# A state-space block with a gated feed-forward on one core: one pair of input terms on GpSimd, ten decay tiles, a moved silu, a transposed residual

## The chip, the cores and the metric

The kernel runs on one core of a Trainium2 chip. The metric is the device time of one launch in microseconds (us); lower is better. Five engines work in parallel, each in its own program order and tied to the others by semaphores: TensorE (PE, matmuls), VectorE (DVE), ScalarE (ACT, activations), GpSimd (POOL), and SyncE (SP), which here only issues DMAs.

## The reference

Input x is 32 sequences of 256 steps with 128 channels, all in float32.

```python
xz = x @ W_in.T                      # 128 -> 512, halves x_ssm and z (256 channels each)
x_ssm = silu(conv4(x_ssm) + conv_b)  # causal, one 4-tap filter for each channel
proj = x_ssm @ W_x.T                 # 16 columns B, 16 columns C, 1 column dt
dt = softplus(proj[..., -1:] * W_dt[:, 0] + b_dt)
h_t = exp(dt_t * A) * h_{t-1} + (x_t * dt_t) * B_t      # 256 channels x 16 states
y_t = sum over states of h_t * C_t, plus x_t * D
attn = (y * silu(z)) @ W_out.T
x1 = layernorm(x + attn)
h = silu(lin(x1, w1)) * lin(x1, w2)  # 128 -> 512
h = gelu(lin(h, h1)); h = gelu(lin(h, h2))              # 512 -> 512, twice
out = layernorm(x1 + lin(h, w3))     # 512 -> 128
```

## The kernel before

**Blocks and rounds.** Two sequences make one block of 512 columns (TB), 16 blocks in all. The program is a software pipeline of 18 rounds j, written out by hand in `rounds` (L212). In round j the scan of block j runs (DVE, POOL, ACT), beside it the front of block j+1 (z, silu of the convolution, rows of B and C, dt), the intake of block j+2 (projection and convolution), the back of block j-1 (output projection, first norm, gate and up, first hidden layer) and the tail of block j-2 (second hidden layer, down projection, second norm). Each engine's `run` walks through 16 visits v and has its instructions hung on a visit; that list is the order of its queue. Rounds 2 to 14 hold every part; round 0 has no back, round 1 no tail, round 15 no front, round 16 no scan, and round 17 is tail alone.

**The scan.** 256 channels times 16 states are 32 tiles u of 128 partitions, two for each visit. A group k is four tiles and takes one load of dt (`dtr`) and one of x*dt (`xdr`), spread from DRAM over the partitions by SP; neighbouring groups share a load, so k=1 and k=3 use the same one, and only the first of them waits for it. B is spread into `brep`, and ACT copies it into the PSUM bank X (`fill_X`, L438), three times in a round. For tile u:
- ACT forms the decay `dA` = exp(dt*A) (`decay`, L425), into a ring of 8 tiles, six tiles ahead of the scan (DA_RING, AHEAD, L33 and L36).
- DVE forms the input term U = X * xdr (L723) in one of two PSUM banks and then scans, h = dA*h + U (L736), into `hb`, a ring of four pairs (the wait on s_p, L731).
- POOL multiplies the pair of `hb` by C into `pb`, also four pairs (`output_term`, L368).
- PE sums four tiles over the states into Y (`sum_group`, L801), once in two visits: group k after visit 2k+1 of POOL, in PE's visit 2k+3.

In round 0 the first three groups take their replicated dt and x*dt from PE (`replicate`, L870, matrix `rep_sb`) and not from DRAM.

**The rest of a round, where the change touches it.** POOL's visit 4 begins with the reciprocal root of the first norm (`rsqrt`, L379), visits 7 and 8 with the products silu(gate)*up (L408, two in each), visits 9, 11 and 12 with the terms of dt (`add_dt`, `times_dt`). DVE's visit 0 has the three taps of the convolution's first half, visit 1 the gate of the former block's second half (it needs PE's sum of group 7), visit 5 x1 (`scaled`, L683), visit 10 the gate of the first half. ACT's visit 1 has two gelus, the start of Y and then `silu_conv` (L456), which needs the silu table and after which the exp/log table is loaded again (L612); visit 3 has the variances of the first norm; visit 6 the silus of the four gates with the copies of the four ups (L633 to L639); visit 7 the copy of the rows and the softplus for dt. PE's visit 4 has `add_x1` (L837), which puts x1T times the centring matrix `cent` into the bank of the down projection, `turn_x1` (L864, transposes of x1) and `down`; visit 6 the first gate and up matmuls; visit 8 `rows_proj` and `dt_proj`, which need the silu of the convolution. `down_last` (L827) does for the last block what `add_x1` and `down` do for the others.

Of the kernel before, what the change touches and what calls it, by code (L numbers as in the profile page):

```python
# [24 lines left out]
GT = 4  # L25
# [4 lines left out]
PARITIES = 2  # L30
LOADS = NC * PARITIES
DT_SLOTS, XD_SLOTS = LOADS, 3
DA_RING = 8  # L33
H_PAIRS = 4
P_PAIRS = 4
AHEAD = 6  # L36
EPS = 1e-5

CW, CB, DP, WD, BD = 0, 4, 5, 6, 7
CHP = 8  # L40


def states_of(k):

    return (0, 0, 1, 1, 1, 1, 0, 0)[k]


def build(nc, xT, win, wx, chp, alog, cwrow, sel, rep, wout, w1, w2, h1, h2, w3, scales, cent_in, ident_in, out):
    with ExitStack() as ctx:
# [20 lines left out]
        sc_sb = sb("sc_sb", [P, 5, NH])  # L70
        negA = sb("negA", [P, TILES])
        sel_sb = sb("sel_sb", [P, PARITIES, 2 * SD])
        rep_sb = sb("rep_sb", [P, PARITIES, P])
        diagD = sb("diagD", [P, NC, P])
        ident, cent = sb("ident", [P, P]), sb("cent", [P, P])
        mhalf, eps = sb("mhalf", [P, NT]), sb("eps", [P, NT])

# [25 lines left out]
        hid = sb("hid", [P, NH, TB])  # L103
        g1 = sb("g1", [P, NH, TB])
        up = g1
        g2 = hid
        yo = sb("yo", [P, NT, DM])
        w3_raw = yo[:].rearrange("p a b -> p (a b)")
# [31 lines left out]
        s_rdt, s_rxd = sem("s_rdt"), sem("s_rxd")  # L140
        s_X, s_start = sem("s_X"), sem("s_start")
        s_dA, s_u, s_h, s_p, s_y = sem("s_dA"), sem("s_u"), sem("s_h"), sem("s_p"), sem("s_y")
        s_gate, s_op = sem("s_gate"), sem("s_op")
        s_var1, s_rs1, s_x1, s_x1t, s_x1c = sem("s_var1"), sem("s_rs1"), sem("s_x1"), sem("s_x1t"), sem("s_x1c")
        s_ga, s_sg, s_up, s_upc, s_hid = sem("s_ga"), sem("s_sg"), sem("s_up"), sem("s_upc"), sem("s_hid")
# [76 lines left out]
        def _(sp):  # L222
# [13 lines left out]
            def spread_B(b, g):  # L236
                if b > 0:
                    sp.wait_ge(s_X, 3 * b - g)
                piece = scr_rows[b % 2, g * SN:(g + 1) * SN, :]
                sp.dma_start(brep[:, g, :], piece.unsqueeze(0).to_broadcast([SD, SN, TB])).then_inc(s_b[g], 16)  # L240

# [8 lines left out]
                    sp.dma_start(o[:, slot, q, :], piece.unsqueeze(1).to_broadcast([SD, SN, TB])).then_inc(s_o[slot][q], 16)  # L250

            load_xT(0)
            sp.dma_start(rep_sb[:], rep).then_inc(s_rep, 16)
            sp.dma_start(wc1[:], cwrow.to_broadcast([P, TAPS * P])).then_inc(s_cw, 16)
            sp.dma_start(wx_sb[:], wx.rearrange("(c p) m -> p c m", p=P)).then_inc(s_wx, 16)
            sp.dma_start(ident[:], ident_in).then_inc(s_ident, 16)
# [36 lines left out]
            def run(j, scan, intake, front, back, tail):  # L293
                I, A, F, T = j + 2, j + 1, j - 1, j - 2
                if scan:
                    if j > 0:
                        sp.wait_ge(s_dA, TILES * j)
                        spread_steps(j, 1, 1, scr_dt, dtr, s_dtr)
                        sp.wait_ge(s_u, TILES * j)
                        spread_steps(j, 1, 0, scr_xd, xdr, s_xdr)  # L300
                    if back:
                        sp.wait_ge(s_op, F + 1)
                    sp.dma_start(xres[:], xT[:, bass.ts(j, TB)]).then_inc(s_xres, 16)
                if intake:
                    sp.wait_ge(s_c1, A + 1)
                    sp.wait_ge(s_z, 2 * A + 2)
                    load_xT(I)
                if scan and j > 0:
                    sp.wait_ge(s_u, TILES * j + 3 * GT)
                    spread_steps(j, 1, 1, scr_xd, xdr, s_xdr)  # L310
                if front:
                    sp.wait_ge(s_rows, A + 1)
                    store_rows(A, range(NT))
                    sp.wait_ge(s_dt, 2 * A + 1)
                    store_steps(A, 0, scr_dt, dts, s_dts)
                    sp.wait_ge(s_xd, 2 * A + 1)
                    store_steps(A, 0, scr_xd, xds, s_xds)
                    sp.wait_ge(s_dts[0], 16 * (A + 1))
                    sp.wait_ge(s_dA, TILES * j + 4 * GT)
                    spread_steps(A, 0, 0, scr_dt, dtr, s_dtr)  # L320
                    sp.wait_ge(s_store, 16 * NT * (A + 1))
                    spread_B(A, 0)
                    sp.wait_ge(s_xds[0], 16 * (A + 1))
                    sp.wait_ge(s_u, TILES * j + 4 * GT)
                    spread_steps(A, 0, 0, scr_xd, xdr, s_xdr)
                    spread_steps(A, 0, 1, scr_dt, dtr, s_dtr)
                    spread_C(A, (0,))
                    sp.wait_ge(s_dt, 2 * A + 2)
                    store_steps(A, 1, scr_dt, dts, s_dts)
                    sp.wait_ge(s_xd, 2 * A + 2)  # L330
                    store_steps(A, 1, scr_xd, xds, s_xds)
                    sp.wait_ge(s_u, TILES * j + 7 * GT)
                    spread_steps(A, 0, 1, scr_xd, xdr, s_xdr)
                    spread_B(A, 1)
                    spread_C(A, (1,))
                if tail:
                    rows_out = out[bass.ts(T, TB), :].rearrange("(t p) m -> p t m", p=P)
                    sp.wait_ge(s_yo, T + 1)
                    if j <= NB:
                        sp.dma_start(rows_out, yo[:]).then_inc(s_out, 16)  # L340
                    else:
                        sp.dma_start(rows_out[:, 0:2, :], yo[:, 0:2, :]).then_inc(s_out, 16)
                        sp.wait_ge(s_yo, T + 2)
                        sp.wait_ge(s_yoa, 1)
                        sp.dma_start(rows_out[:, 2:4, :], yo[:, 2:4, :]).then_inc(s_out, 16)
                if front:
                    sp.wait_ge(s_dts[1], 16 * (A + 1))
                    sp.wait_ge(s_dA, TILES * j + 7 * GT)
                    spread_steps(A, 1, 0, scr_dt, dtr, s_dtr)
                    sp.wait_ge(s_xds[1], 16 * (A + 1))  # L350
# [5 lines left out]
        def _(pool):  # L356
# [11 lines left out]
            def output_term(b, v):  # L368
# [3 lines left out]
                if v >= P_PAIRS or b > 0:  # L372
# [3 lines left out]
                nc.gpsimd.tensor_tensor(pb[:, qs:qs + 2, :], hb[:, hs:hs + 2, :],  # L376
                                        crep[:, b % 2, g:g + 1, :].to_broadcast([P, 2, TB]), ALU.mult).then_inc(s_p, 1)

            def rsqrt(var, ve, rs, s_var, n_var, s_rs, n_rs, ts=slice(0, NT)):  # L379
                pool.wait_ge(s_var, n_var)  # L380
                nc.gpsimd.tensor_tensor(ve[:, ts], var[:, ts], eps[:, ts], ALU.add).then_inc(s_rs, 1)
                pool.wait_ge(s_rs, n_rs - 1)
                nc.gpsimd.tensor_tensor(rs[:, ts], ve[:, ts], mhalf[:, ts], ALU.pow).then_inc(s_rs, 1)
# [12 lines left out]
            def run(j, scan, intake, front, back, tail):  # L396
                I, A, F, T = j + 2, j + 1, j - 1, j - 2
                for v in range(STEPS):
# [16 lines left out]
                        add_dt(A, 1)  # L415
                    if v == 12 and front:
                        times_dt(A, 1)
                    if scan:
                        output_term(j, v)

# [3 lines left out]
        def _(act):  # L424
            def decay(b, u):  # L425
# [6 lines left out]
                    act.wait_ge(s_dtr[slot][q], 16 * loads_up_to(b, k, DT_SLOTS))  # L432
                if u >= DA_RING or b > 0:
                    act.wait_ge(s_h, TILES * b + u - DA_RING + 1)
                nc.scalar.activation(halves(dA[:, u % DA_RING, :])[:, :, 1:SEQ], halves(BREP[q] if by_product(b, k) else dtr[:, slot, q, :])[:, :, 1:SEQ],  # L435
                                     ACT.Exp, scale=negA[:, u:u + 1]).then_inc(s_dA, 1)

            def fill_X(b, i):  # L438

                g = i % 2  # L440
                if i < 2:
                    act.wait_ge(s_b[g], 16 * (b + 1))
                if b > 0 or i > 0:
                    act.wait_ge(s_u, TILES * b + (0, 2 * GT, 6 * GT)[i])
                nc.scalar.activation(X[:], brep[:, g, :], ACT.Copy).then_inc(s_X, 1)  # L445

            def conv_first(b):
# [112 lines left out]
            def run(j, scan, intake, front, back, tail):  # L560
# [3 lines left out]
                for v in range(STEPS):  # L564
# [41 lines left out]
                        copy_z(A, 0)  # L606
                    if v == 4 and tail:
                        gelu(g2, 3, BH2, s_h2, s_g2, T, (2, 3))
                    if v == (1 if back else 5) and front:
                        silu_conv(A, 0)  # L610
                        silu_conv(A, 1)
                        act.preload_act_table_set("natural_log_exp_and_others")  # L612
# [5 lines left out]
                    if v == 6:  # L618
# [4 lines left out]
                        if j == NB + 1:  # L623
# [6 lines left out]
                                    last.then_inc(s_var2, 1)  # L630
                            act.wait_ge(s_rs2, 2 * T + 4)
                            nc.scalar.activation(yo[:, 3, :], BLAST[3][:, 0:P], ACT.Copy, scale=rs2[:, 3:4]).then_inc(s_yoa, 1)
                        for m in range(NH) if back else ():  # L633
                            act.wait_ge(s_ga, 4 * F + 1 + m)
                            nc.scalar.activation(hid[:, m, :], BGATE[m], ACT.Silu,  # L635
# [27 lines left out]
        def _(dve):  # L663
# [37 lines left out]
            def run(j, scan, intake, front, back, tail):  # L701
                I, A, F, T = j + 2, j + 1, j - 1, j - 2
                for v in range(STEPS):
                    if scan:
# [6 lines left out]
                            dve.wait_ge(s_X, 2)  # L711
                        elif v in (0, 4, 12):
                            dve.wait_ge(s_X, 3 * j + 1 + (0, 4, 12).index(v))
                        for i in range(2):
                            if v > 0 or j > 0:
                                dve.wait_ge(s_h, TILES * j + 2 * v + i - 1)
                            if by_product(j, k):
# [14 lines left out]
                        for i in range(2):  # L732
                            u = 2 * v + i
                            dve.wait_ge(s_dA, TILES * j + u + 1)
                            dve.wait_ge(s_u, TILES * j + u + 1)
                            nc.vector.tensor_tensor_scan(hb[:, 2 * (v % H_PAIRS) + i, :], dA[:, u % DA_RING, :], U[i][:],  # L736
                                                         0.0, ALU.mult, ALU.add).then_inc(s_h, 1)
                    if v == 4 and j == 0:
                        taps(1)
# [19 lines left out]
        def _(pe):  # L759
# [66 lines left out]

            def down_last(b):  # L827
                for t in range(NT):
                    nc.tensor.matmul(BLAST[t][:, 0:P], tile_of(x1T[:], t), cent[:], start=True, stop=False, skip_group_check=True)
                pe.wait_ge(s_g2, 4 * b + 4)  # L830
                for t in range(NT):
                    for k in range(NH):
# [4 lines left out]
            def add_x1(b):  # L837

                pe.wait_ge(s_g2, 4 * b + 3)
                for t in range(NT):  # L840
                    nc.tensor.matmul(tile_of(BW3, t), tile_of(x1T[:], t), cent[:], start=(t == 0), stop=False, skip_group_check=True)

            def down(b):
                pe.wait_ge(s_w3c, 1)
# [238 lines left out]
```

## Time and profile before

| | |
|---|---|
| runs shown | 1063.3, 1059.74, 1062.15 us (median 1062.15) |
| profiled execution, its own time | 1063.54 us |
| span in the profile | 1061.7 us, 13755 instructions, so 1.8 us lie around it |
| busy, share of the span | PE 95%, DVE 90%, ACT 86%, POOL 75% |
| mean granted TensorE clock | 0.969 of full speed |
| table loads on ACT | 1283 ns each |
| DMA | 184 MB, mean 173 GB/s |

A busy share is a mean over the launch. PE's times are modelled at their ends: two matmuls in a row overlap a little in the records, so a merged row of the timeline is a little longer than the distance to the next row's start. The work of a stretch is best read from start to start. A row `[1.33 <-POOL pb L376]` says how long the engine had stood idle before the row and who, by the profile, released it; where an instruction waits for several semaphores the named one is only the last by the profile.

### The profile page before, as it was taken

The numbers are of one execution on the slowest core, as the hardware profiler recorded it, in microseconds if no ns is written. First come the engines' busy times: TensorE is split into PE (matmuls) and PEld (weight loads), VectorE is DVE, ScalarE is ACT, GpSimd is POOL, SyncE is SP. The second block draws the span as 40 slices with busy tenths as digits, with TensorE's granted clock in tenths as the row PEclk, the third lists the DMA queues.
The fourth block names the chain that finished last, engine by engine and source line by source line (L and its number), as shares of the span: only waits on it lengthen the run. The fifth ranks groups of instructions, "written<-read, shape, count | busy, mean of one in ns | idle before, by whom it ended". The sixth has DMA issues, their size and how long they took to land.

```text
span 1061.7 us, 13755 instructions
## 1 busy us (share of the span) xinstructions
PE 1006.7 (95%) x4000; PEld 457.4 (43%) x4000; DVE 952.1 (90%) x1143; ACT 909.6 (86%) x1519; POOL 796.1 (75%) x455
## 2 busy tenths in 40 slices
PE   5947999999999999999999999999999999999998
PEld 2313335353444535353443535344453535335454
DVE  1899999999999999999999999999999999999500
ACT  5396798999999999999999999999999999996442
POOL 1476877969787896969788796978789696977520
PEclk8677899999999999999999999999999999998999
DMA  4959294764939286583929377482928658391000
GB/s 128 280 183 285 66 282 121 220 209 122 258 97 300 85 248 179 164 249 101 295 63 300 117 225 204 132 248 94 316 71 246 181 172 233 98 295 50 1 10 11
DMA packets 110428, 184.14 MB, mean 173 GB/s; under 512 B 12944, under 2 KB 23696, under 8 KB 110352
## 3 DMA queue, kind: packets, MB, share of 16 engines
q1 hardware_dynamic: 109824, 182.94, 59.2%
q8 instruction: 32, 0.52, 0.2%
q14 instruction: 44, 0.36, 0.1%
q10 hardware_dynamic: 528, 0.32, 0.1%
HBM read 161.19 MB, written 22.02 MB: 173 GB/s over the span
## 4 chain that ended last, share of the span: by engine, by line
PE 56%; POOL 14%; issue 13%; DVE 9%; ACT 7%; DMA 0%; POOLq 0%; ACTq 0%; SPq 0%; DVEq 0%
PE G L818 21%; PE Y L809 7%; POOL pb L376 6%; PE G L848 5%; PE G L769 5%; DVE hb L736 5%; PE Y L818 5%; POOL hid L408 3%; DVE U L723 3%; PE G L822 3%; PE Y L860 2%; ACT dA L435 2%; POOL dts L359 2%; POOL xds L366 2%; PE G L825 1%
## 5 line engine op out<-in xcount | busy, mean ns | idle before, releaser
L376 POOL TENSOR_TENSOR pb<-hb,crep 128x1024 f32<-128x1024 f32 x256 | 603.2, 2365 | 177.6 <-DVE hb L736 154.3
L736 DVE TENSOR_TENSOR_SCAN hb<-dA,U 128x512 f32<-128x512 f32 x512 | 594.5, 1203 | 21.1 <-POOL pb L376 18.5
L435 ACT ACTIVATE dA<-dtr,negA 128x510 f32<-128x510 f32 x500 | 320.8, 711 | 1.6 <-DVE hb L736 1.1
L723 DVE TENSOR_TENSOR U<-X,xdr 128x512 f32<-128x512 f32 x500 | 318.3, 683 | 0.7 <-ACT X L445 0.7
L818 PE MATMUL G<-g,h_sb 128*128 128x512 f32 x512 | 234.2, 601 | 0.0
L818 PE MATMUL G<-hid,h_sb 128*128 128x512 f32 x384 | 173.1, 601 | 0.8 <-ACT g L638 0.8
L809 PE MATMUL Y<-pb,sel_sb 128*32 128x512 f32 x1024 | 139.1, 615 | 17.6 <-POOL pb L376 17.6
L818 PEld LDWEIGHTS G<-g,h_sb 128*128 128x128 f32 x512 | 93.5, 190 | 138.2 <-issue 136.5
L818 PEld LDWEIGHTS G<-hid,h_sb 128*128 128x128 f32 x384 | 70.4, 190 | 103.8 <-issue 101.9
L408 POOL TENSOR_TENSOR hid<-hid,g 128x512 f32<-128x512 f32 x64 | 80.8, 1274 | 14.6 <-ACT g L638 14.6
L809 PEld LDWEIGHTS Y<-pb,sel_sb 128*32 128x32 f32 x1024 | 20.7, 109 | 96.8 <-issue 71.9
L769 PE MATMUL G<-xT_sb,wc 128*128 128x512 f32 (+3 forms) x120 | 58.6, 634 | 2.8 <-ACT w_sb L592 2.3
L517 ACT ACTIVATE hid<-G,sc_sb 128x512 f32<-128x512 f32 x64 | 42.4, 686 | 20.9 <-PE G L818 20.4
L517 ACT ACT_TABLE_LOAD x45 | 57.7, 1283 | 0.8
L848 PE MATMUL G<-w_sb,hid 128*128 128x128 f32 x480 | 58.2, 281 | 0.0
L818 PE MATMUL Y<-hid,h_sb 128*128 128x512 f32 x128 | 57.5, 592 | 0.0
L848 PEld LDWEIGHTS G<-w_sb,hid 128*128 128x128 f32 x480 | 57.1, 198 | 0.0
L635 ACT ACTIVATE hid<-G,sc_sb 128x512 f32<-128x512 f32 x48 | 32.9, 686 | 26.8 <-PE G L822 26.8
L822 PE MATMUL G<-x1T,w_sb 128*128 128x512 f32 x96 | 51.5, 619 | 0.0
L359 POOL TENSOR_TENSOR dts<-dts,xds 128x512 f32<-128x512 f32 x30 | 38.2, 1274 | 4.8 <-ACT xds L491 4.7
L366 POOL TENSOR_TENSOR xds<-dts,xs 128x512 f32<-128x512 f32 x31 | 39.5, 1275 | 1.3
L435 ACT ACT_TABLE_LOAD x31 | 39.8, 1283 | 0.6
(136 smaller groups left out, 1135.2 us busy)
## 6 DMA issues: line engine op xcount, KB each, us to landing
dtr<-scr_dt SPq DMA_DIRECT2D x252, 256.0 KB, 7.3
xdr<-scr_xd SPq DMA_DIRECT2D x252, 256.0 KB, 6.6
brep<-scr_rows SPq DMA_DIRECT2D x32, 256.0 KB, 5.7
crep<-scr_rows SPq DMA_DIRECT2D x32, 256.0 KB, 7.9
scr_dt<-dts SPq DMA_DIRECT2D x32, 256.0 KB, 4.0
scr_xd<-xds SPq DMA_DIRECT2D x32, 256.0 KB, 4.0
xres<-xT_d SPq DMA_DIRECT2D x16, 256.0 KB, 2.9
xT_sb<-xT_d SPq DMA_DIRECT2D x15, 256.0 KB, 2.9
```

What stands on the lines that cost most here:

```text
L366: nc.gpsimd.tensor_tensor(xds[:, c, :], dts[:, c, :], xs[:, b % 2, c, :], ALU.mult).then_inc(s_xd, 1)
L376: nc.gpsimd.tensor_tensor(pb[:, qs:qs + 2, :], hb[:, hs:hs + 2, :], crep[:, b % 2, g:g + 1, :].to_broadcast([P, 2, TB]), ALU.mult).then_in ...
L408: nc.gpsimd.tensor_tensor(hid[:, m, :], hid[:, m, :], up[:, m, :], ALU.mult).then_inc(s_hid, 1)
L435: nc.scalar.activation(halves(dA[:, u % DA_RING, :])[:, :, 1:SEQ], halves(BREP[q] if by_product(b, k) else dtr[:, slot, q, :])[:, :, 1:SEQ ...
L517: nc.scalar.activation(o[:, m, :], banks[m], ACT.Gelu, scale=sc_sb[:, kind, m:m + 1]).then_inc(s_done, 1)
L723: nc.vector.tensor_tensor(U[i][:], X[:], xdr[:, slot, q + i, :], ALU.mult).then_inc(s_u, 1)
L736: nc.vector.tensor_tensor_scan(hb[:, 2 * (v % H_PAIRS) + i, :], dA[:, u % DA_RING, :], U[i][:], 0.0, ALU.mult, ALU.add).then_inc(s_h, 1)
L769: last = nc.tensor.matmul(halves(bank_c1(b))[:, :, s:SEQ], wc1[:, TAPS - 1 - s, :], halves(x_of(b))[:, :, 0:SEQ - s], start=(s == 0), stop ...
L809: last = nc.tensor.matmul(Y[c][rows32, :], sel_sb[:, e, :], pb[:, (GT * k + q) % (2 * P_PAIRS), :], start=False, stop=(k % (GROUPS // NC) ...
L818: last = nc.tensor.matmul(to, w[:, k, m * P:(m + 1) * P], x[:, k, :], start=(k == 0), stop=(k == NH - 1))
L822: nc.tensor.matmul(BGATE[m], w1_sb[:, m * P:(m + 1) * P], x1T[:], start=True, stop=True).then_inc(s_ga, 1)
L848: last = nc.tensor.matmul(tile_of(BW3, t), tile_of(g2[:, k, :], t), w3_sb[:, k, :], start=False, stop=(k == NH - 1), skip_group_check=True)
```

## The change

GpSimd takes over the input terms of pair 7 (tiles 14 and 15, group 3): in its visit 4 it multiplies that pair of `xdr` by `brep` in place, and VectorE scans from `xdr` in SBUF where it otherwise scans from the PSUM bank U. The count of s_u is therefore 30 for each round (`terms_up_to`), and a new semaphore s_ub counts the pair. The ring of decays has ten tiles, and ACT works eight tiles ahead. The SBUF for this comes from `diagD` and `rep_sb`, which are only used at the start and now lie in `g1`. `silu_conv` moves, in rounds with a back, from ACT's visit 1 to visit 6, ahead of the four gates' silus; its own reload of the exp/log table goes. `add_x1` and `down_last` put x1 itself into the bank, as a transpose of x1T against `ident`, where they put x1 times `cent`.

```diff
-DA_RING = 8
+DA_RING = 10
...
-AHEAD = 6
+AHEAD = 8
+
+POOL_V = 7
...
+def terms_up_to(b, u):
+
+    return (TILES - 2) * b + u - (2 if u > 2 * POOL_V else 0)
+
+
+def decay_slot(b, u):
+    return (TILES * b + u) % DA_RING
...
-        rep_sb = sb("rep_sb", [P, PARITIES, P])
-        diagD = sb("diagD", [P, NC, P])
...
+        diagD = g1[:, 0, 0:NC * P].rearrange("p (c m) -> p c m", c=NC)
+        rep_sb = g1[:, 1, 0:PARITIES * P].rearrange("p (e m) -> p e m", e=PARITIES)
...
             def spread_B(b, g):
                 if b > 0:
                     sp.wait_ge(s_X, 3 * b - g)
+                    if g == states_of(POOL_V // 2):
+                        sp.wait_ge(s_ub, b)
...
-                    sp.wait_ge(s_u, TILES * j + 4 * GT)
+                    sp.wait_ge(s_u, terms_up_to(j, 4 * GT))
+                    sp.wait_ge(s_h, TILES * j + 4 * GT)
                     spread_steps(A, 0, 0, scr_xd, xdr, s_xdr)
...
+            def input_terms(b):
+
+                k, q = divmod(2 * POOL_V, GT)
+                slot, g = slot_of(b, k, XD_SLOTS), states_of(k)
+                pool.wait_ge(s_b[g], 16 * (b + 1))
+                for i in range(2):
+                    pool.wait_ge(s_xdr[slot][q + i], 16 * loads_up_to(b, k, XD_SLOTS))
+                pool.wait_ge(s_u, terms_up_to(b, 2 * POOL_V - 2 * GT + 2))
+                nc.gpsimd.tensor_tensor(xdr[:, slot, q:q + 2, :], xdr[:, slot, q:q + 2, :], brep[:, g:g + 1, :].to_broadcast([P, 2, TB]),
+                                        ALU.mult).then_inc(s_ub, 1)
...
+                    if v == 4 and scan:
+                        input_terms(j)
                     if scan:
                         output_term(j, v)
...
-                nc.scalar.activation(halves(dA[:, u % DA_RING, :])[:, :, 1:SEQ], halves(BREP[q] if by_product(b, k) else dtr[:, slot, q, :])[:, :, 1:SEQ],
+                nc.scalar.activation(halves(dA[:, decay_slot(b, u), :])[:, :, 1:SEQ], halves(BREP[q] if by_product(b, k) else dtr[:, slot, q, :])[:, :, 1:SEQ],
...
-                    if v == (1 if back else 5) and front:
+                    if v == 5 and front and not back:
                         silu_conv(A, 0)
                         silu_conv(A, 1)
                         act.preload_act_table_set("natural_log_exp_and_others")
...
+                        if front and back:
+                            silu_conv(A, 0)
+                            silu_conv(A, 1)
                         for m in range(NH) if back else ():
                             act.wait_ge(s_ga, 4 * F + 1 + m)
...
-                        for i in range(2):
+                        for i in range(2) if v != POOL_V else ():
...
                             dve.wait_ge(s_dA, TILES * j + u + 1)
-                            dve.wait_ge(s_u, TILES * j + u + 1)
-                            nc.vector.tensor_tensor_scan(hb[:, 2 * (v % H_PAIRS) + i, :], dA[:, u % DA_RING, :], U[i][:],
+                            if v != POOL_V:
+                                dve.wait_ge(s_u, terms_up_to(j, u + 1))
+                            elif i == 0:
+                                dve.wait_ge(s_ub, j + 1)
+                            nc.vector.tensor_tensor_scan(hb[:, 2 * (v % H_PAIRS) + i, :], dA[:, decay_slot(j, u), :],
+                                                         xdr[:, slot, q + i, :] if v == POOL_V else U[i][:],
                                                          0.0, ALU.mult, ALU.add).then_inc(s_h, 1)
...
-                    nc.tensor.matmul(BLAST[t][:, 0:P], tile_of(x1T[:], t), cent[:], start=True, stop=False, skip_group_check=True)
+                    nc.tensor.matmul(BLAST[t][:, 0:P], tile_of(x1T[:], t), ident[:], is_transpose=True, start=True, stop=False,
+                                     skip_group_check=True)
...
-                    nc.tensor.matmul(tile_of(BW3, t), tile_of(x1T[:], t), cent[:], start=(t == 0), stop=False, skip_group_check=True)
+                    nc.tensor.matmul(tile_of(BW3, t), tile_of(x1T[:], t), ident[:], is_transpose=True, start=(t == 0), stop=False,
+                                     skip_group_check=True)
```

The other lines of the diff put `terms_up_to` where a count of s_u was written as TILES * j + u.

## Rows read from the trace of the kernel before

**Rows 1.** Windows by stretch: engines' busy us (instructions), PEclk, DMA share, GB/s; one round.

```profile
544.90:605.60 60.70, 60.28 (x250) 27.44 (x247) 59.30 (x72) 56.93 (x97) 49.74 (x29) 1.00 0.62 188
```

**Rows 2.** Groups by line, whole launch: xcount | busy us, mean ns | idle before, releasers.

```profile
L376 POOL TENSOR_TENSOR pb<-hb,crep 128x1024 f32<-128x1024 f32 x256 | 603.2, 2365 | 177.6 <-DVE hb L736 154.3 <-PE Y L809 23.1
```

**Rows 3.** Chain that ended last, one round apart: start us, us, what.

```profile
543.96 0.70 ACT g L638
...
604.67 0.70 ACT g L638
```

**Rows 4.** Timeline of PE, one period: start us, us, line, tile, count [idle before].

```profile
559.48 1.07 PE L809 MATMUL Y<-pb,sel_sb 128*32 128x512 f32 x8 [0.30 <-POOL pb L376]
...
581.06 1.07 PE L809 MATMUL Y<-pb,sel_sb 128*32 128x512 f32 x8
...
594.62 1.05 PE L841 MATMUL G<-cent,x1T 128*128 128x128 f32 x8
...
595.78 0.66 PE L867 MATMUL Y<-ident,x 128*128 128x128 f32 x4
```

**Rows 5.** Timeline of POOL, the same period.

```profile
544.79 1.27 POOL L408 TENSOR_TENSOR hid<-hid,g 128x512 f32<-128x512 f32 x1 [0.39 <-ACT g L638]
...
598.11 2.37 POOL L376 TENSOR_TENSOR pb<-hb,crep 128x1024 f32<-128x1024 f32 x1 [1.48 <-DVE hb L736]
...
601.52 2.36 POOL L376 TENSOR_TENSOR pb<-hb,crep 128x1024 f32<-128x1024 f32 x1 [1.04 <-DVE hb L736]
...
603.84 1.29 POOL L408 TENSOR_TENSOR hid<-hid,g 128x512 f32<-128x512 f32 x1
```

**Rows 6.** Timeline of DVE, the same period.

```profile
554.63 2.33 DVE L736 TENSOR_TENSOR_SCAN hb<-dA,U 128x512 f32<-128x512 f32 x2 [1.33 <-POOL pb L376]
...
573.96 1.27 DVE L723 TENSOR_TENSOR U<-X,xdr 128x512 f32<-128x512 f32 x2
...
583.01 0.67 DVE L681 TENSOR_TENSOR gT<-Y,zs 128x512 f32<-128x512 f32 x1
...
595.04 0.68 DVE L686 TENSOR_TENSOR x<-Y,rs 128x512 f32<-128x512 f32 x1
...
601.29 1.27 DVE L723 TENSOR_TENSOR U<-X,xdr 128x512 f32<-128x512 f32 x2
```

**Rows 7.** Timeline of ACT, the same period.

```profile
553.83 2.54 ACT L435 ACTIVATE dA<-dtr,negA 128x510 f32<-128x510 f32 x4
...
572.11 0.58 ACT L445 ACTIVATE X<-brep 128x512 f32<-128x512 f32 x1
...
582.46 1.28 ACT L461 ACT_TABLE_LOAD   x1
...
584.92 1.28 ACT L612 ACT_TABLE_LOAD   x1
...
602.10 0.69 ACT L635 ACTIVATE hid<-G,sc_sb 128x512 f32<-128x512 f32 x1 [1.21 <-PE G L822]
```

**Rows 8.** Waits of the queue of SP, two rounds: us in total, times, longest us.

```profile
SPq L228 <- ACT rows L476: 28.6, 2, 14.3
```

**Rows 9.** Timeline of DVE in round 0.

```profile
69.68 2.33 DVE L736 TENSOR_TENSOR_SCAN hb<-dA,U 128x512 f32<-128x512 f32 x2 [2.63 <-issue]
```

**Rows 10.** Timeline of ACT in round 0.

```profile
44.22 0.78 ACT L449 ACTIVATE conv<-G,chp_sb 128x512 f32<-128x512 f32 x1 [4.17 <-PE G L762]
...
68.88 2.54 ACT L435 ACTIVATE dA<-dtr,negA 128x510 f32<-128x510 f32 x4
```

**Rows 11.** Timeline of PE in round 15.

```profile
957.83 1.11 PE L867 MATMUL Y<-ident,x 128*128 128x128 f32 x4 [1.28 <-DVE x L686]
...
958.74 5.92 PE L848 MATMUL G<-w_sb,hid 128*128 128x128 f32 x32
```

**Rows 12.** Chain that ended last, in round 16, TensorE at full clock.

```profile
1012.18 0.89 PE G L841 x8
...
1013.07 0.44 PE Y L867 x4
```

More of the change, by code:

```diff
@@ L142, in build @@
         s_dA, s_u, s_h, s_p, s_y = sem("s_dA"), sem("s_u"), sem("s_h"), sem("s_p"), sem("s_y")
+        s_ub = sem("s_ub")
         s_gate, s_op = sem("s_gate"), sem("s_op")
@@ L252, in _ @@
             load_xT(0)
-            sp.dma_start(rep_sb[:], rep).then_inc(s_rep, 16)
+            sp.dma_start(rep_sb, rep).then_inc(s_rep, 16)
             sp.dma_start(wc1[:], cwrow.to_broadcast([P, TAPS * P])).then_inc(s_cw, 16)
@@ L298, in run @@
                         spread_steps(j, 1, 1, scr_dt, dtr, s_dtr)
-                        sp.wait_ge(s_u, TILES * j)
+                        sp.wait_ge(s_u, terms_up_to(j, 0))
                         spread_steps(j, 1, 0, scr_xd, xdr, s_xdr)
@@ L308, in run @@
                 if scan and j > 0:
-                    sp.wait_ge(s_u, TILES * j + 3 * GT)
+                    sp.wait_ge(s_u, terms_up_to(j, 3 * GT))
                     spread_steps(j, 1, 1, scr_xd, xdr, s_xdr)
@@ L331, in run @@
                     store_steps(A, 1, scr_xd, xds, s_xds)
-                    sp.wait_ge(s_u, TILES * j + 7 * GT)
+                    sp.wait_ge(s_u, terms_up_to(j, 7 * GT))
                     spread_steps(A, 0, 1, scr_xd, xdr, s_xdr)
@@ L443, in fill_X @@
                 if b > 0 or i > 0:
-                    act.wait_ge(s_u, TILES * b + (0, 2 * GT, 6 * GT)[i])
+                    act.wait_ge(s_u, terms_up_to(b, (0, 2 * GT, 6 * GT)[i]))
                 nc.scalar.activation(X[:], brep[:, g, :], ACT.Copy).then_inc(s_X, 1)
```

## The prediction

> **What bounds the kernel now.** I read first the stretches of one period. From round 2 to round 14 every 60.70 us hold the same work: PE is busy 60.28, DVE 59.30, ACT 56.93, POOL 49.74, at full TensorE clock [rows 1]. So two engines are nearly full and a saving on one alone is worth little. The chain that ended last gives the pitch: the same copy of an up projection stands at 543.96 and at 604.67, 60.71 us apart [rows 3].
>
> Then the timelines, engine by engine; the period shown runs from visit 7 of one round to visit 6 of the next. PE has two real gaps in it: 0.30 us before the sum of group 4, which waits for POOL, and before the transposes of x1: `add_x1` starts at 594.62 and needs 0.89 [rows 12], so PE is free at 595.51, and the transposes start at 595.78, when x1 has come: 0.27 us [rows 4]. DVE has one gap, 1.33 us before the scans of visit 10. The trace names POOL, but that visit's two decays are the first of the four that start on ACT at 553.83, behind the rows and the first softplus; the first ends at about 554.5, the scans start at 554.63 [rows 6, 7]. The reader is to see that this wait is for decays. POOL waits for scans before outputs 5 and 6 (1.48 and 1.04) and then works without a pause from visit 7 to the sum's wait at 559.48, but for 0.39 us in which it waits for ACT [rows 4, 5]. ACT waits 1.21 us for PE's first gate matmul [rows 7].
>
> **The change part by part, in the middle rounds.**
>
> *Input terms on POOL.* DVE loses two of 32 multiplications, 1.2 us start to start (601.29 to the next scan, of the 1.27 shown) [rows 6]. POOL gains one instruction of the shape of an output term, 2.37 us [rows 2], ahead of output 4. Its operands are there: group 3 uses the load that group 1 used, and the terms of visit 3 are older than output 3. Behind it stand outputs 4 to 6 and the products of visit 7. The waits before outputs 5 and 6 sum to 2.52 us, so they take the 2.37; output 6 then ends near 603.9 as before, which is where the first product starts (603.84) [rows 5]. Cost nothing, by 0.15 us; if this cover goes, the products are late, and with them the sum of group 4.
>
> *Ten decay tiles.* The decays of visit 10 are now issued in visit 6, ahead of gates and softplus. DVE's 1.33 us go. DVE could then be 2.5 us ahead of today. It won't keep it: next round's first terms (573.96) need X, filled by ACT at 572.11 to 572.69, which leaves 1.3; the gate at 583.01 needs PE's last sum, 581.06 to 582.13, which leaves 0.9 [rows 4, 6, 7]. That is the lead with which DVE comes to x1 (595.04), and 0.27 is all that PE waits there. What DVE saves, 2.5 us, thus turns into new waits of DVE, but for 0.27 us.
>
> *The silu of the convolution.* Gone from visit 1: one table load, 1.28; the exp/log load after it stays, since decays follow gelus. The two silus, from 583.74 to 584.92, go behind the silu table's load in visit 6: 1.18 us into a wait of 1.21 [rows 7]. ACT reaches the variances after the output projection early and waits there for PE, so from there to the gates it is exactly as late as today. Cost nothing, with 0.03 us to spare. Late if it isn't: the silus of the gates, the products on POOL, group 4. The readers of the silu, rows and dt, come in visit 8, behind all the gates.
>
> *x1 turned back.* Eight records at 0.89 us for the four products with `cent` become four transposes; turning x1 costs 0.44 us for four [rows 12]. Between 0.44 and 0.89, I take 0.44: same shape, same form. PE saves 0.45 us in every round with a tail.
>
> *The rest.* SP's new wait on s_h for visit 7's scans stands before the load of x*dt for the next block; SP stands there only after `store_rows`, for which it waits 14.3 us a round, until the rows are copied at about 551, when those scans are over [rows 8]: nothing. The wait on s_ub is older still. Moving two constants into `g1` costs nothing, it is first written in round 1. In round 0, the first convolution copy has two more decays ahead of it, 1.3 us, and waits 4.17 us for PE there [rows 10].
>
> So PE's two gains are on the path: 0.45 + 0.27 = 0.72 us a period, 60.71 to 59.99, for 13 periods **9.4 us**. The 0.30 before group 4 stays: POOL's chain to it starts at the up copy and is untouched. If ACT keeps up, that chain starts 0.72 sooner, with PE: ACT can do its four gate instructions 0.6 us apart where PE now feeds them every 0.86, so it makes good 0.8.
>
> **Start and end.** Rounds 0 and 1 are bound by DVE up to round 1's visit 6. There the wait for decays is 2.63 us [rows 9] and goes, and 1.2 for the terms goes too, 3.8 in all. But the next pair's scans, today at 69.68 + 2.24 + 1.18 = 73.1, need the first of the decays that start at 68.88 [rows 10], at 69.6 at the earliest: **3.5 us**.
> In round 15 PE waits for x1 (1.28), and DVE is 1.3 ahead there, having no taps or early gate to wait for: **1.3 us**. The transposes of rounds 16 and 17 give 2 x 0.45 = **0.9 us**. An upper end: PE's idle time before x1 is followed by a down projection at half clock, 5.92 for 32 records [rows 11] where the same takes 3.7 at full clock; if the clock stayed up, 2.8 us more with the transposes'.
>
> Sum: 9.4 + 3.5 + 1.3 + 0.9 = 15.1. The profiled execution took 1063.54, so 1048.4; it lies 1.4 above the median of the runs shown, so I say 1048.
>
> **A row that isn't there: the scans of visit 7.** They will read both dA and xdr from SBUF, while POOL reads `hb` and `crep`. In the trace of before, each DVE instruction beside POOL's work has at most one input in SBUF, the other in PSUM. A price has to be bounded: at the lower end nothing; at the upper each scan stops POOL for its own length, 2.3 us for the two, and DVE waits in turn for one POOL term, 2.37. I take nothing in the sum, the nearest row being the scan with one input in SBUF, which runs beside POOL's terms at its full 2.33 for two [rows 6], and keep the upper end as a rival. The Trainium skill (SBUF — State Buffer, "Who interferes with whom") speaks against the change here: a VectorE instruction with two SBUF inputs and a GpSimd instruction that reads SBUF block one another for a whole instruction. By that rule the price is the upper end; no row of before can show it.
>
> **Rivals.**
>
> 1. *The port.* DVE starts the instruction behind scan 6 at 601.29, POOL its output 6 at 601.52 [rows 5, 6]: the scans of visit 7 come first, each time. If POOL stands for both, 2.3 us, output 6 ends 2.3 later; only 0.4 us is left before the second product, so group 4 comes 1.9 later. Per period 1.9 - 0.72 = +1.2; 13 periods 15.6, one more 1.9 in round 1, less 5.7 at start and end: +11.8, 1075. If POOL stands for one scan, +0.1 a period: 1060. It decides from about 1.1 us of POOL's time a period. For: the placing just before POOL's tight stretch. Against: nothing but that the block may be shorter than an instruction.
> 2. *ACT or POOL sets the pitch.* The covers are 0.03 us (silus) and 0.15 (input terms). If either is short by some tenths, the products start as late as today, PE's 0.72 becomes a longer wait before group 4, and only start and end remain: 1063.5 - 5.7 = 1058, 1054 to 1061. For: margins thinner than a semaphore's delay. Against: the 0.8 that ACT can make good.
> 3. *It doesn't do what it says.* The transposes cost what the products cost, and DVE's lead is lost elsewhere: 1063.5 - 4 = 1060; or both ends lose their lead also: no change.
>
> **How the numbers follow.** My forecast 0.47 (1043 to 1053: the lower end has the clock of round 15, and 0.1 us a period), rival 1 0.25 (a third of it with one scan blocked, the rest 1066 to 1078), rival 2 0.20, rival 3 0.08. A measurement of this kernel can tell about 0.3%, 3.2 us, from no change, so faster means under 1059. Faster: 0.47 + 0.13 of rival 2 + 0.04 of rival 1 + 0.02 = 0.66; within: 0.07 + 0.04 + 0.05 = 0.16; slower: 0.18, nearly all rival 1. The range 1042 to 1070 leaves out half of rival 1 and the tails of the first case; the forecast's own is 1043 to 1053.
>
> **What would show it.** The chain: a pitch of 60.0 (60.7 rival 2, 61.9 rival 1). PE: `add_x1` four records in 0.44, no gap before the transposes, 0.30 before group 4. DVE: no wait before visit 10, but new ones before the first terms (X) and the gate. POOL: an instruction of 2.37 in visit 4, first product on time; a pause or an output 6 over 2.4 us beside the scans of visit 7 would be rival 1. ACT: 15 table loads fewer, one wait of some 2.4 us before the variances, none before the gates. A pitch above 60.4 makes the forecast wrong.

## The result, and the profile after

The changed kernel took 1065.79 us (1065.41 to 1066.71, 5 runs) against 1061.7 for the kernel before (5 runs): ratio 1.0036, interval 1.0025 to 1.0048. It is slower by 0.36%, where 1048 was forecast; the time lies inside the wide range of 1042 to 1070, which takes in part of rival 1, and outside the forecast's own 1043 to 1053. The profiled execution has a span of 1063.6 us, 1.9 more than before.

The stretch that answers to [rows 1], and the busy totals from the page:

```profile
PE 991.9 (93%) x3936; PEld 445.8 (42%) x3936; DVE 967.2 (91%) x1111; ACT 887.0 (83%) x1502; POOL 855.6 (80%) x471
```

```profile
544.90:605.60 60.70, 59.16 (x242) 26.75 (x234) 59.91 (x70) 55.29 (x94) 53.14 (x29) 1.00 0.68 188
```

PE lost work and is busy 1.12 us less in a stretch of the same length; DVE lost two multiplications and is busy 0.61 us more. The costliest groups of the changed kernel say where (columns as in [rows 2]):

```profile
L392 POOL TENSOR_TENSOR pb<-hb,crep 128x1024 f32<-128x1024 f32 x256 | 613.5, 2411 | 129.1 <-DVE hb L771 93.8
L771 DVE TENSOR_TENSOR_SCAN hb<-dA,U 128x512 f32<-128x512 f32 x480 | 556.9, 1202 | 0.0
...
L435 POOL TENSOR_TENSOR hid<-hid,g 128x512 f32<-128x512 f32 x64 | 93.1, 1474 | 8.8 <-ACT g L670 8.6
L771 DVE TENSOR_TENSOR_SCAN hb<-dA,xdr 128x512 f32<-128x512 f32 x32 | 69.7, 2222 | 0.0
```

A scan from U takes 1202 ns, a scan from xdr 2222. POOL's output terms and products, which were 2365 and 1274 ns long before, are longer too: the products are busy 93.1 us where they were busy 80.8, and the output terms 613.5 where they were busy 603.2 [rows 2].

DVE's timeline of one period, then POOL's, beside the scans of visit 7:

```profile
601.47 1.20 DVE L771 TENSOR_TENSOR_SCAN hb<-dA,U 128x512 f32<-128x512 f32 x1
602.58 1.20 DVE L771 TENSOR_TENSOR_SCAN hb<-dA,xdr 128x512 f32<-128x512 f32 x1
...
603.69 3.33 DVE L771 TENSOR_TENSOR_SCAN hb<-dA,xdr 128x512 f32<-128x512 f32 x1
...
606.94 0.67 DVE L755 TENSOR_TENSOR U<-X,xdr 128x512 f32<-128x512 f32 x1
```

```profile
595.55 2.37 POOL L403 TENSOR_TENSOR xdr<-xdr,brep 128x1024 f32<-128x1024 f32 x1
597.88 4.70 POOL L392 TENSOR_TENSOR pb<-hb,crep 128x1024 f32<-128x1024 f32 x2
602.81 3.12 POOL L392 TENSOR_TENSOR pb<-hb,crep 128x1024 f32<-128x1024 f32 x1 [0.23 <-DVE hb L771]
605.90 2.18 POOL L435 TENSOR_TENSOR hid<-hid,g 128x512 f32<-128x512 f32 x1
```

The reader is to see a hand-over, told in records and not in waits. The first scan from xdr runs from 602.58 to 603.78 at its normal 1.20. Output 6 is issued at 602.81 and lasts 3.12: counted back from its end, 605.93, its normal 2.36 begin at 603.57, near the first scan's end. The second scan is issued at 603.69 and ends at 607.02: its last 1.1 us come after output 6. The first product is issued at 605.90 and lasts 2.18, its normal 1.27 begin at 606.81. Whichever of the two began first runs to its end; the other's record is stretched by the wait. POOL loses 0.76 + 0.91 = 1.67 us a period, DVE 2.13.

What it does to PE, one period apart in the chain, then in PE's timeline, with DVE's gate between:

```profile
500.39 1.06 PE Y L845 x8
...
561.56 1.06 PE Y L845 x8
```

```profile
561.56 1.06 PE L845 MATMUL Y<-pb,sel_sb 128*32 128x512 f32 x8 [1.53 <-POOL pb L392]
...
583.14 1.06 PE L845 MATMUL Y<-pb,sel_sb 128*32 128x512 f32 x8
...
596.70 0.60 PE L878 MATMUL G<-ident,x1T 128*128 128x128 f32 x4
597.13 0.60 PE L905 MATMUL Y<-ident,x 128*128 128x128 f32 x4
597.57 3.74 PE L886 MATMUL G<-w_sb,hid 128*128 128x128 f32 x32
```

```profile
584.27 0.69 DVE L713 TENSOR_TENSOR gT<-Y,zs 128x512 f32<-128x512 f32 x1 [0.32 <-PE Y L845]
```

The pitch is 61.17 us, 0.46 longer. The wait before the sum of group 4 grew from 0.30 to 1.53 [rows 4]. The rest of the forecast is there: the transposes take 0.43 and no gap stands before the transposes of x1. DVE has no wait before visit 10 any more [rows 6]; new short ones stand before the next round's first terms (0.40, ACT's X) and before the gate (0.32, PE). On ACT the first gate's silu follows the moved silus without a wait.

The loop that now sets the pitch runs through three engines, none of which waits inside its part of it. PE goes from the sum of group 4 (561.56) to the sum of group 7 (583.14), DVE from its gate, which waits for that sum (584.27), to the scans for which output 6 waits (602.81), and POOL from there to the next sum of group 4, 61.17 us after the first. In the kernel before the same loop has room in two places: the gate starts 1.95 us after the start of group 7's sum [rows 4, 6] where it can start 1.13 after it, and POOL waits 0.39 for ACT [rows 5]. Without this 0.82 and 0.39 it is 59.5 us long. PE's transposes (596.70, 597.13) and the wait for x1 lie outside it. Below, "POOL's loop" is this loop.

By stretches of the span, with the sum of group 4 as the mark in rounds 1 and 14, and beside it run b of below, which has no such scan:

| | before | changed | b_psum_scan |
|---|---|---|---|
| start to round 1's mark | 134.13 | 133.48 | 130.56 |
| 13 periods | 789.61 | 795.05 | 778.91 |
| round 14's mark to the end | 137.96 | 135.07 | 136.33 |
| span | 1061.7 | 1063.6 | 1045.8 |

### The profile page after: what moved, and what is told of

Read it like the earlier page. It is cut to its first block, busy times and chain, and to the rows that moved or that the text cites. A ratio compares the mean times of both kernels' runs of the same rounds, so it can differ in the third digit from the quotient of the medians.

```text
span 1063.6 us, 13622 instructions
## 1 busy us (share of the span) xinstructions
PE 991.9 (93%) x3936; PEld 445.8 (42%) x3936; DVE 967.2 (91%) x1111; ACT 887.0 (83%) x1502; POOL 855.6 (80%) x471
## 4 chain that ended last, share of the span: by engine, by line
PE 45%; issue 17%; ACT 16%; POOL 13%; DVE 7%; DMA 0%; POOLq 0%; ACTq 0%; SPq 0%; DVEq 0%
PE G L854 22%; POOL hid L435 6%; POOL pb L392 5%; PE Y L845 5%; PE G L805 5%; PE Y L854 5%; DVE hb L771 4%; ACT dA L464 4%; PE Y L898 2%; DVE U L755 2%; ACT L464 2%; POOL dts L375 2%; ACT L490 1%; ACT L546 1%; ACT xs L490 1%
## 5 line engine op out<-in xcount | busy, mean ns | idle before, releaser
L392 POOL TENSOR_TENSOR pb<-hb,crep 128x1024 f32<-128x1024 f32 x256 | 613.5, 2411 | 129.1 <-DVE hb L771 93.8
L771 DVE TENSOR_TENSOR_SCAN hb<-dA,U 128x512 f32<-128x512 f32 x480 | 556.9, 1202 | 0.0
L755 DVE TENSOR_TENSOR U<-X,xdr 128x512 f32<-128x512 f32 x468 | 298.0, 682 | 6.0 <-ACT X L474 6.0
L435 POOL TENSOR_TENSOR hid<-hid,g 128x512 f32<-128x512 f32 x64 | 93.1, 1474 | 8.8 <-ACT g L670 8.6
L771 DVE TENSOR_TENSOR_SCAN hb<-dA,xdr 128x512 f32<-128x512 f32 x32 | 69.7, 2222 | 0.0
L546 ACT ACTIVATE hid<-G,sc_sb 128x512 f32<-128x512 f32 x64 | 42.4, 686 | 25.1 <-PE G L854 24.8
```

Of the source, the lines that this page charges most:

```text
L435: nc.gpsimd.tensor_tensor(hid[:, m, :], hid[:, m, :], up[:, m, :], ALU.mult).then_inc(s_hid, 1)
L546: nc.scalar.activation(o[:, m, :], banks[m], ACT.Gelu, scale=sc_sb[:, kind, m:m + 1]).then_inc(s_done, 1)
L755: nc.vector.tensor_tensor(U[i][:], X[:], xdr[:, slot, q + i, :], ALU.mult).then_inc(s_u, 1)
```

## The experiments

Ten kernels ran, all timed in turn with the kernel before.

**Theory: the port.** A DVE scan with two SBUF inputs and a POOL instruction that reads SBUF exclude one another; all else of my working holds. ("The port" is short for this exclusion. The runs show that it happens, not what in the chip makes it.) **Rivals:** POOL's longer program makes group 4 late; or ACT's stretch from the output projection to the gates does.

**b_psum_scan.** The changed kernel, scans of pair 7 from PSUM:

```diff
-                                                         xdr[:, slot, q + i, :] if v == POOL_V else U[i][:],
+                                                         U[i][:],
```

> The changed kernel, but the scans of pair 7 read the PSUM banks U (old contents, so the states of that pair are another function's) in place of xdr in SBUF; GpSimd still forms the terms and VectorE still waits for them. It separates the port from GpSimd's longer program. Port theory: scans of that pair back at 2.3 us for two from 4.44, GpSimd's output term beside them back at 2.37 from 3.12 and the two products at 2.5 from 3.43, the wait before the sum of group 4 back near 0.3 from 1.53, pitch 60.0, 1047 to 1052. Rival, GpSimd's 2.37 us more is what makes group 4 late: time stays at 1062 to 1066.

1047.38 us (1046.85 to 1047.55), ratio 0.9863 (0.9848 to 0.9878). Groups of this run, and PE's timeline:

```profile
L392 POOL TENSOR_TENSOR pb<-hb,crep 128x1024 f32<-128x1024 f32 x256 | 601.6, 2364 | 126.9 <-DVE hb L771 90.7 <-PE Y L845 36.1 <-issue 0.2
L771 DVE TENSOR_TENSOR_SCAN hb<-dA,U 128x512 f32<-128x512 f32 x512 | 592.3, 1200 | 0.4 <-ACT dA L464 0.4
L435 POOL TENSOR_TENSOR hid<-hid,g 128x512 f32<-128x512 f32 x64 | 80.8, 1274 | 13.7 <-ACT g L670 12.4
```

```profile
549.97 1.07 PE L845 MATMUL Y<-pb,sel_sb 128*32 128x512 f32 x8 [0.28 <-POOL pb L392]
```

All durations are back, though POOL still forms the terms. The mark before stands at 490.06: a pitch of 59.91. The pair's states are wrong in this run, its instructions are those of the changed kernel. One operand's place costs some 18 us (1065.79 against 1047.38), and POOL's extra 2.37 us a period cost nothing. Both rivals fall.

**c_port_only.** The reverse, on the kernel before (with the wait of SP on s_h that the changed kernel has, so that xdr is not overwritten early):

```diff
-                            nc.vector.tensor_tensor_scan(hb[:, 2 * (v % H_PAIRS) + i, :], dA[:, u % DA_RING, :], U[i][:],
+                            nc.vector.tensor_tensor_scan(hb[:, 2 * (v % H_PAIRS) + i, :], dA[:, u % DA_RING, :], xdr[:, slot, q + i, :] if v == 7 else U[i][:],
```

> The kernel before with one edit: the scans of pair 7 read xdr in SBUF and not U (the product with B is left out of that pair's states, while VectorE still forms it). GpSimd has no instruction more. Port theory: two scans take over 4 us and the GpSimd instructions beside them gain 1 to 1.7 us, the pitch goes from 60.71 to 61.7 to 62.4, 1073 to 1085 us. Rival, two SBUF inputs cost only where GpSimd is full: 1062 to 1066.

1076.37 us (1075.66 to 1076.63), ratio 1.0136 (1.0120 to 1.0151). DVE's and POOL's timelines of this run:

```profile
548.00 4.63 DVE L737 TENSOR_TENSOR_SCAN hb<-dA,xdr 128x512 f32<-128x512 f32 x2
```

```profile
547.04 2.35 POOL L377 TENSOR_TENSOR pb<-hb,crep 128x1024 f32<-128x1024 f32 x1 [1.04 <-DVE hb L737]
549.48 4.23 POOL L409 TENSOR_TENSOR hid<-hid,g 128x512 f32<-128x512 f32 x2
```

Here DVE still multiplies before the scans, so output 6 is under way when they are issued: it keeps its 2.35, the first scan waits for it, and the two products, 2.50 alone, pay 1.73. One by one, the scans take 2.48 and 2.23 and the products 2.07 and 2.19: scan and product take turns. The order of issue says who pays. The pitch is 61.61 (567.11 to 628.72 in the chain), just under the 61.7 expected, and DVE is full, busy 60.63 of 60.70 us: its 59.30 of [rows 1] and the 2.31 us by which its scans are longer sum to 61.61.

**i_port_idle.** From a_no_terms (below), two SBUF inputs where POOL is idle:

```diff
-                                                         U[i][:],
+                                                         xdr[:, slot, q + i, :] if v == 1 and j > 0 else U[i][:],
```

> Run a_no_terms with one edit: from round 1 on the scans of pair 1 read xdr in SBUF and not U (the product with B is left out of that pair's states, VectorE still forms it). In visit 1 GpSimd has ended output 0 and waits for just these scans. Theory, two SBUF inputs cost only beside a GpSimd instruction that reads SBUF: the two scans take 2.3 to 2.6 us, pitch 59.9, 1047 to 1051 us. Rival, a scan with two SBUF inputs is slower by itself: 4.4 us for two, pitch 60.5 or more.

1050.17 us (1049.47 to 1051.33), ratio 0.9896 (0.9881 to 0.9911), against 0.9879 (0.9864 to 0.9894) of a_no_terms: the intervals overlap. DVE's and POOL's timelines:

```profile
569.91 1.29 DVE L750 TENSOR_TENSOR U<-X,xdr 128x512 f32<-128x512 f32 x2
571.11 2.97 DVE L763 TENSOR_TENSOR_SCAN hb<-dA,xdr 128x512 f32<-128x512 f32 x2
```

```profile
569.52 2.36 POOL L389 TENSOR_TENSOR pb<-hb,crep 128x1024 f32<-128x1024 f32 x1 [2.26 <-PE Y L837]
574.22 2.36 POOL L389 TENSOR_TENSOR pb<-hb,crep 128x1024 f32<-128x1024 f32 x1 [2.34 <-DVE hb L763]
```

The size I gave, at most 2.6, was missed by a little: 2.97. Output 0 ended at 571.88; from there to 574.08 are 2.2 us, the normal time of two scans. The scan is not slower by itself; it waited 0.77 us (571.11 to 571.88) for the last POOL instruction and then ran alone.

**a_no_terms.** The changed kernel without GpSimd's part (`input_terms`, s_ub, the skipped multiplications):

```diff
-                    if v == 4 and scan:
-                        input_terms(j)
...
-                        for i in range(2) if v != POOL_V else ():
+                        for i in range(2):
...
-                                                         xdr[:, slot, q + i, :] if v == POOL_V else U[i][:],
+                                                         U[i][:],
```

> The changed kernel with pair 7's input terms back on VectorE (from X and xdr into U); ring of ten, moved silu and transposes stay. Port theory: GpSimd's terms and VectorE's scan from SBUF are what costs, so the other three parts show their worth: a pitch of 60.0 to 60.2 us, 1047 to 1053 us, 0.8 to 1.3% faster than the kernel before. Rival, ScalarE's dense stretch from the output projection to the gates sets the pitch: then this version is slow too, pitch 60.7 or more, 1058 to 1062.

1049.02 us (1048.51 to 1049.56), ratio 0.9879 (0.9864 to 0.9894): 1.2% less time than before, with nothing of the function left out. Its timeline of PE:

```profile
551.62 1.07 PE L837 MATMUL Y<-pb,sel_sb 128*32 128x512 f32 x8 [0.29 <-POOL pb L389]
```

The mark before stands at 491.70, the pitch is 59.92, as in run b and a little under the 60.0 expected. So offloading the terms would be worth only 1.6 us even without the port (1049.02 against 1047.38), and all of it at the start: round 2's mark stands at 192.11 here and at 190.47 in b. In the middle rounds PE sets the pitch, and DVE's 1.2 us a period have nobody waiting for them.

**d_terms_only.** The other three parts taken back, GpSimd's part left.

```diff
-DA_RING = 10
+DA_RING = 8
...
-AHEAD = 8
+AHEAD = 6
...
-                    if v == 5 and front and not back:
+                    if v == (1 if back else 5) and front:
```

(and `cent` for the transposes.)

> The changed kernel with the ring of eight, the silu in visit 1 and the products with cent as before, so that only the input terms on GpSimd (and the two constants in g1) are left of the change. Port theory: it loses the 0.7 us a period that the transposes and the earlier x1 give, and with it the start: pitch 61.9, 1073 to 1080 us. Rival, the silu in visit 6 is what makes the products late: then this is no slower than the changed kernel, 1060 to 1066.

1068.68 us (1068.30 to 1069.72), ratio 1.0067 (1.0048 to 1.0086). Missed: the port theory had 1073 or more. Timeline of PE:

```profile
563.99 1.06 PE L842 MATMUL Y<-pb,sel_sb 128*32 128x512 f32 x8 [1.08 <-POOL pb L392]
```

The mark before stands at 502.83: a pitch of 61.16, that of the changed kernel. PE's gains don't add to the port's price, they vanish in it: the loop through PE, DVE and POOL sets the pitch, the transposes lie outside it, and what PE saves only lengthens its wait, from 1.08 to 1.53.

**e_moved.** POOL forms pair 5, in its visit 2, where it has time. The main lines (the counts of s_u and s_ub follow from them):

```diff
-POOL_V = 7
+POOL_V = 5
...
-                    if v == 4 and scan:
+                    if v == 2 and scan and j > 0:
                         input_terms(j)
...
                     sp.wait_ge(s_u, terms_up_to(j, 3 * GT))
+                    sp.wait_ge(s_h, TILES * j + 3 * GT)
```

> The changed kernel with the pair moved: GpSimd forms the input terms of pair 5 in its visit 2, where it waits for scans anyway, and VectorE scans that pair from SBUF in visit 5, beside output term 4, behind which GpSimd has 1.5 us to spare (in round 0 VectorE forms them, since that group has no load there). Theory, the port costs GpSimd some 0.8 us and VectorE one output term here too, but neither is late for the sum of group 4: pitch 59.9 to 60.1, 1046 to 1051 us. Rival, the block delays the scans of visit 6 and with them output 6 and the products: pitch 60.5 or more, 1055 to 1062.

1053.43 us (1052.93 to 1054.60), ratio 0.9924 (0.9908 to 0.9941), between the two expectations. DVE, POOL and PE of this run:

```profile
590.23 0.69 DVE L718 TENSOR_TENSOR x<-Y,rs 128x512 f32<-128x512 f32 x1 [0.39 <-POOL rs L410]
590.84 3.88 DVE L771 TENSOR_TENSOR_SCAN hb<-dA,xdr 128x512 f32<-128x512 f32 x2
```

```profile
590.17 2.36 POOL L392 TENSOR_TENSOR pb<-hb,crep 128x1024 f32<-128x1024 f32 x1
594.87 2.37 POOL L392 TENSOR_TENSOR pb<-hb,crep 128x1024 f32<-128x1024 f32 x1 [2.34 <-DVE hb L771]
```

```profile
556.17 1.06 PE L845 MATMUL Y<-pb,sel_sb 128*32 128x512 f32 x8 [0.69 <-POOL pb L392]
```

POOL isn't stretched at all here, only DVE, by 1.57; but output 5 waits for the scan, and through it the products are late: a pitch of 60.32 (495.85 to 556.17). The part that was to be free is dearer than none (a_no_terms).

**h_no_ring.** a_no_terms with DA_RING = 8 and AHEAD = 6.

> Run a_no_terms with the ring of eight decays, six ahead, as before. VectorE then carries all input terms and waits for the decays of visit 10, 1.3 us a period. My working gave the ring nothing in the middle rounds but the lead of VectorE before x1. Theory: VectorE is full with that wait (59.3 + 1.3), the pitch is 60.6 to 60.7 and the time 1058 to 1062, so the ring carries the gain with the terms left on VectorE. Rival, the transposes alone lower the pitch to 60.2: 1052 to 1055.

1061.25 us (1060.34 to 1062.52; ratio 0.9998, 0.9988 to 1.0008; the mark at 498.25 and 558.96, 60.71 apart): no change against before, though transposes and moved silu are in it. DVE, then PE:

```profile
554.12 2.33 DVE L763 TENSOR_TENSOR_SCAN hb<-dA,U 128x512 f32<-128x512 f32 x2 [1.34 <-POOL pb L389]
```

```profile
595.27 0.66 PE L897 MATMUL Y<-ident,x 128*128 128x128 f32 x4 [0.57 <-DVE x L713]
```

The wait for decays is back, and PE's saving has become a wait for x1, 0.57 where it was 0.27.

**f_no_transpose, g_no_silu, j_ring_only.** a_no_terms with the products with `cent` (f), with `silu_conv` in visit 1 (g), and with both, which leaves the kernel before with ten decay tiles (j).

> Run a_no_terms with the products of x1T with cent in place of the transposes. With the ring of ten TensorE sets the pitch, so its 0.45 us must show in full: pitch 60.3 to 60.4 from 59.92, 1055 to 1057 us. Rival, VectorE still sets it and the transposes are worth nothing: 1048 to 1051.

> Run a_no_terms with the silu of the convolution in ScalarE's visit 1 as before. Theory: ScalarE waited for TensorE at the gates by 1.2 us, and with a pitch lower by 0.8 it waits 0.4 still; decays come 2.4 us later after visit 1, which the ring of ten covers: no change from a_no_terms, 1047 to 1051. Rival, ScalarE then sets the pitch: 60.3 to 60.7, 1054 to 1060.

> The kernel before with the ring of ten decays, eight ahead, and nothing else of the change but the two constants in g1. Since the moved silu was worth nothing beside the other parts: as f_no_transpose, pitch 60.3 to 60.4, 1055 to 1057 us, 0.5 to 0.7% faster than before. Rival, without the moved silu ScalarE is late for the variances again and holds x1: 1058 to 1062.

f: 1054.09 us (1053.83 to 1054.39), ratio 0.9929 (0.9911 to 0.9947); only its time is used, so its pitch is not known. g: 1048.04 (1046.24 to 1049.49), 0.9874 (0.9858 to 0.9891), pitch 59.92 (491.44 to 551.36). j: 1053.34 (1052.98 to 1053.93), 0.9923 (0.9906 to 0.9941); its mark:

```profile
494.23 1.06 PE L834 MATMUL Y<-pb,sel_sb 128*32 128x512 f32 x8 [0.29 <-POOL pb L389]
...
554.62 1.07 PE L834 MATMUL Y<-pb,sel_sb 128*32 128x512 f32 x8 [0.30 <-POOL pb L389]
```

A pitch of 60.39. Both f and j came out under their expected times, by 0.9 and 1.7 us. The ring is worth 0.32 us a period, 7.7 us in all; the transposes some 5 us more (f against a) and 0.47 a period (j against a, which differ in the silu's place too), but only with the ring; the silu's place nothing that can be told (g and a overlap).

## Why the prediction was wrong

**The step that failed** is the one of the row that wasn't there: "I take nothing in the sum". The scans of visit 7 and POOL exclude one another, and it costs 1.26 us a period (61.17 against 59.91) and 2.9 at the start (changed kernel against run b). The end is 1.3 us shorter than b's, 1.2 of it by TensorE's clock: from x1's transposes to the sum behind the down projection, in round 15, the changed kernel takes 5.79 us (961.39 to 967.18) and b 6.99 (942.33 to 949.32), at a mean granted clock of 0.71 and 0.58 of full speed; why the grants differ is open. I chose the lower bound because the nearest row, a scan with one input in SBUF, ran at full speed. That row couldn't speak for two inputs: it was near in shape and not in what mattered. The rule of the Trainium skill (SBUF — State Buffer, "Who interferes with whom") said what happened: the runs agree with it, in that the later instruction waits until the earlier one has ended (2.18 for a product of 1.27, 3.33 for a scan of 1.20), and in that the order of issue says who waits.

**Rival 1** had the place and the order of the two instructions right, and its size was off: POOL was to lose 2.3 us and lost 1.67, because the first 0.23 of the scan fell into a wait and the second scan did not hold on but let output 6 go first. It also took PE's 0.72 off a price to which they don't belong, and gave POOL 0.4 us of room where its loop has 1.21 (0.82 before the gate, 0.39 before the product). POOL's loop without the port is 59.5 us, worked out above from the rows of before; PE's is 59.91. The pitch is the larger of the two, not a sum, as d_terms_only shows: 59.5 and 1.67 are the measured 61.17. Rival 1's own sum with 1.67 would give 61.26, close to it, but in part by luck, since its two errors nearly cancel.

**The rest of the sum** held, by run b: start 3.6 us (3.5 forecast), 13 periods 10.7 (9.4), end 1.6 (2.2); the time 1047.4 against 1048. Of the periods' gain of 0.82 us, 0.08 more than the two terms and the 0.02 of the wait before group 4 is spread too thin to name. At the end PE's wait for x1 in round 15, which was to go, grew from 1.28 [rows 11] to 1.73, in the changed kernel and in b:

```profile
961.39 0.66 PE L905 MATMUL Y<-ident,x 128*128 128x128 f32 x4 [1.73 <-DVE x L718]
```

```profile
942.33 1.12 PE L905 MATMUL Y<-ident,x 128*128 128x128 f32 x4 [1.73 <-DVE x L718]
```

x1 did come 1.23 us sooner (32.86 us after the mark of round 14 in both, 34.09 before), near the 1.3 forecast; the wait is longer by the 0.45 that the transposes save before it, which is thus worth nothing in this round.

**The ring** was costed at a lead worth 0.27 us a period. That is what it adds by itself (0.32 in run j), but it is also the condition of the transposes: without it DVE, with all its terms, is full (59.3 and the wait of 1.34, in a pitch of 60.7), and they are worth nothing (h). I had named DVE as nearly full and then costed PE's 0.45 as if PE alone set the pitch; that came out only because the ring was part of the same change.

**The silu** cost nothing and brought nothing, as forecast; rival 2 is excluded by run b. The covers held: the first gate's silu came without delay, the first product was late only by the port. Little is left, though: in b POOL waits 0.25 us for the copy of the first up. ACT's wait before the variances is 1.13 us in both kernels, where 2.4 was forecast, and 17 table loads are gone, where 15 were. The constants in `g1` show nowhere in a_no_terms and b, SP's waits nowhere in b.

Rival 3's doubt on the transposes falls: 0.43 us for four records.

## What to carry to other kernels

Before an operand moves from PSUM to SBUF, ask what the other inputs of that instruction are and what GpSimd does at that moment; a free engine's help can be undone by where it leaves its result. When no row shows a resource, don't take the bound of the nearest row that lacks it. And where two engines are nearly full, compute each one's loop and take the larger: a saving on one is worth nothing until the other has room, and a price on a third counts only above it.

## What the runs showed of the hardware

- Two 512-column scans with both inputs in SBUF took 2.2 us where GpSimd was idle (i_port_idle, from 571.88 on), and up to 4.63 beside it (c_port_only); a GpSimd instruction beside them was longer by 0.76 to 0.92 us, or by nothing where it came first (e_moved). No run has another kind of VectorE instruction with two SBUF inputs, nor a GpSimd instruction that reads no SBUF. Blocked time stands inside the record of the blocked instruction, as busy time; no wait names it. A group with more than one duration for one shape is the sign.
- Four float32 128x128 transposes, to whose results ordinary products are then added in the same PSUM bank, take 0.43 us on TensorE, half of four products of the same shape (0.89 [rows 12]).
- In the changed kernel an activation follows its table load at once: load at 601.68 for 1.28 us, silu at 602.98.
